# Layer 1: turning the softmax probabilities on VectorE and spreading them on ScalarE, in place of spread, TensorE turn and copy

## The reference, cut to what matters

```
x + _L1_attn_ref(_layernorm(x), w_qkv, b_qkv, w_o, b_o):
    q, k, v = split(x @ w_qkv.T + b_qkv)                # 8 heads, width 32
    scores = einsum('bhfc,bhtc->bhft', k, q)            # the key's rows f against the query's rows t
    scores = where(causal, scores, -10000)
    attn = softmax(scores, axis=-2)                     # over f
    vals = einsum('bhft,bhfc->bhtc', attn, v)
    out = vals @ w_o.T + b_o
```

## Time and profile before

| what | us |
|---|---|
| median of 3 runs | 2140.99 (2138.29 to 2141.76) |
| the profiled execution, its own time | 2136.47 |
| its span, first to last instruction | 2134.4 |
| PE busy | 2059.4 (96%) |
| DVE busy | 1308.7 (61%) |
| ACT busy | 683.7 (32%) |
| POOL busy | 248.3 (12%) |

### The profile page before, as it was taken

How to read it: one execution, slowest core, us unless ns; L and a number is a source line. 1 busy time by engine, 2 the same in 40 slices (tenths; PEclk the granted TensorE clock), 3 DMA queues, 4 the chain that set the end, 5 groups by cost and what they waited for, 6 DMA issues and landing times. The chain is left out here.

```text
span 2134.4 us, 33623 instructions
## 1 busy us (share of the span) xinstructions
PE 2059.4 (96%) x10660; PEld 1480.4 (69%) x10660; DVE 1308.7 (61%) x4451; ACT 683.7 (32%) x1861; POOL 248.3 (12%) x360
## 2 busy tenths in 40 slices
PE   7999999999999999999999999999899999779998
PEld 5778677777767778677777867777566666466665
DVE  3736547484654747456483755747577777677885
ACT  2333333333332433333242433333223223122222
POOL 0000000000000000000000000000233333133332
PEclk9999999999999999999999999999999999889999
DMA  7101000010000101001010000120100000000000
GB/s 289 31 15 31 23 24 30 24 30 24 24 20 24 30 24 30 24 24 30 14 37 16 30 23 24 30 86 1 45 1 1 1 0 29 0 1 21 21 15 25
DMA packets 51991, 62.14 MB, mean 29 GB/s; under 512 B 14193, under 2 KB 47665, under 8 KB 51042
## 3 DMA queue, kind: packets, MB, share of 16 engines
q1 hardware_dynamic: 51938, 61.46, 9.1%
HBM read 54.00 MB, written 4.29 MB: 27 GB/s over the span
## 5 line engine op out<-in xcount | busy, mean ns | idle before, releaser
L345 PE MATMUL psLane<-hid,WkT 128*128 128x289 f32 x1536 | 404.0, 408 | 0.0
L352 PE MATMUL psLane<-WvT,hid 128*128 128x384 f32 x1024 | 348.7, 486 | 0.0
L345 PEld LDWEIGHTS psLane<-hid,WkT 128*128 128x128 f32 x1536 | 284.1, 190 | 72.7
L352 PEld LDWEIGHTS psLane<-WvT,hid 128*128 128x128 f32 x1024 | 189.8, 190 | 109.7
L537 ACT ACTIVATE probs<-psLane,nmax 128x289 f32<-128x289 f32 x256 | 126.2, 498 | 423.6 <-DVE nmax L640 423.6
L505 ACT ACTIVATE KT<-psLane 96x289 f32<-96x289 f32 (+2 forms) x384 | 155.8, 406 | 153.3 <-PE psLane L345 151.0
L298 POOL TENSOR_TENSOR tails<-probs,unit 128x66 f32<-128x66 f32 x128 | 38.1, 297 | 1387.3 <-ACT probs L537 1387.3
L678 DVE MAX8 top<-work 128x8 f32<-128x257 f32 x512 | 180.3, 414 | 2.7
L335 PE MATMUL psLane<-xnT,WqT 128*128 128x128 f32 x1536 | 176.6, 275 | 0.0
L335 PEld LDWEIGHTS psLane<-xnT,WqT 128*128 128x128 f32 x1536 | 174.8, 192 | 0.3
L663 DVE TENSOR_TENSOR X<-X,psLane 128x512 f32 (+1 forms) x16 | 11.0, 689 | 261.6 <-PE psLane L417 261.6
(11 more groups left out here) (190 smaller groups left out, 3138.2 us busy)
## 6 DMA issues: line engine op xcount, KB each, us to landing
hid<-in_ctxT SPq DMA_DIRECT2D x64, 514.0 KB, 3.8
y<-X SPq DMA_DIRECT2D x16, 256.0 KB, 2.0
X<-in_x SPq DMA_DIRECT2D x1, 3840.0 KB, 14.9
WqT<-in_WqT SPq DMA_DIRECT2D x4, 768.0 KB, 11.4
WoT<-in_WoT SPq DMA_DIRECT2D x1, 3072.0 KB, 21.7
Vtail<-Vlat SPq DMA_DIRECT2D x128, 24.0 KB
w_qkv<-in_w_qkv SPq DMA_DIRECT2D x2, 1536.0 KB, 6.5
w_ffn<-in_w_ffn SPq DMA_DIRECT2D x2, 1024.0 KB, 8.0
```

The lines of the kernel that those rows point to most:

```text
L345: mm = pe.matmul(out[:, 0:S], WkT[:, c, P * k:P * k + P], hid[:, j, c, :], start=(c == 0), stop=(c == DC - 1))
L352: mm = pe.matmul(out[:, 0:KW], hid[:, j, c, P * s:P * s + P], WvT[:, c, :], start=(c == 0), stop=(c == DC - 1))
```

## The change: what it does

`turn_probs` is now DVE's last step: after the scaling it turns `p` (128x256) into the new buffer `turned` by DVE's transpose, which turns each 32x32 block by itself. As every batch and head is such a block, this is the turn that is needed. `spread_p` is now ACT's: four ACTIVATEs with function Copy and a scale of one number for each partition (a column of `jmask`) write `turned` to the block diagonal of `pT`. The eight turns of L1434 on PE, the four multiplies of L1562 on DVE and the copy of L1485 on ACT are gone. `values` takes over the wait for `v_ready`; `gate` waits for `s_filled` (the scores have read lane buffer 0) in place of `pt_filled`; DVE's `turn_probs` waits for `pt_ready` of the tile four earlier, which has read `turned`. In `SLOTS1`, `turn_probs` has DVE's old place 2.461, `spread_p` has 2.571, `values` has 2.769 in place of 2.919, and `evac_pt` is gone.

```diff
--- before.py
+++ after.py
@@ -850,7 +850,7 @@
     "gate": 0.000, "add_rest": 0.027, "mix": 0.173, "turn_mix": 0.485, "add_mix": 0.614, "stats1": 0.707,
     "rstd1": 0.773, "rows1": 0.929, "bias": 2.451, "turn1": 0.989, "xnT1": 1.045, "qkv": 1.310,
     "evac_qk": 1.590, "evac_v": 1.762, "spread_k": 1.808, "scores": 2.006, "mask": 2.056, "shift": 2.136,
-    "exps": 2.342, "spread_p": 2.461, "turn_probs": 2.571, "evac_pt": 2.710, "values": 2.919, "evac_ot": 2.919,
+    "exps": 2.342, "turn_probs": 2.461, "spread_p": 2.571, "values": 2.769, "evac_ot": 2.919,
     "project": 3.015, "add_proj": 3.074, "stats2": 3.162, "rstd2": 3.245, "rows2": 3.395, "turn2": 3.500,
     "xnT2": 3.539, "ffn": 3.877, "add_ffn": 3.989, "store": 3.989,}
 
@@ -1342,19 +1342,19 @@
         QK = sb("lane_QK", [P, LANES, 4, P])
         V = sb("lane_V", [P, LANES, EW])
         p = sb("lane_p", [P, LANES, EW])
+        turned = sb("lane_turned", [P, LANES, EW])
         gate = sb("gate1", [P, 1])
 
         n4, n5 = norm_sems(sem, "n4"), norm_sems(sem, "n5")
         names = ("gated", "gate_added", "mixed", "mix_turned", "mix_added", "bias_added", "qkv_filled", "v_ready",
                  "qk_ready", "kd_ready", "s_filled", "s_kept", "s_masked", "max_done", "s_shifted", "p_ready",
-                 "sum_done", "rinv_ready", "pd_ready", "pt_filled", "pt_ready", "av_filled", "p_scaled",
+                 "sum_done", "rinv_ready", "p_turned", "pt_ready", "av_filled", "p_scaled",
                  "ot_ready", "proj_filled", "proj_added", "ffn_filled", "ffn_added")
         s = {k: sem(f"l1_{k}") for k in names}
         out_done = sem("out_done")
 
         mixed = lambda u: lanes[:, u, 0, 0:D]
         Kd = lambda u: lanes[:, u, 0].rearrange("p (a j h k) -> p a j h k", a=2, j=TB, h=4)
-        Pd = lambda u: lanes[:, u, 0].rearrange("p (h j k) -> p h j k", h=EH, j=TB)
         pT = lambda u: lanes[:, u, 1]
         OT = lambda u: xnT[:, u, 0:EW // P]
         low = lambda u: ps[:, u, 0:512]
@@ -1427,15 +1427,9 @@
                                        Kd(u)[:, half, j], start=True, stop=True, tile_position=(0, L * j))
                 mm.then_inc(s["s_filled"], 1)
 
-            def turn_probs(t, u):
-                pe.wait_ge(s["pd_ready"], t + 1)
-                pe.wait_ge(s["v_ready"], t + 1)
-                for h in range(EH):
-                    mm = pe.transpose(ps[:, u, P * h:P * h + P], Pd(u)[:, h].rearrange("p j k -> p (j k)"), ident[:])
-                mm.then_inc(s["pt_filled"], 1)
-
             def values(t, u):
                 pe.wait_ge(s["pt_ready"], t + 1)
+                pe.wait_ge(s["v_ready"], t + 1)
                 for h in range(EH):
                     n, at = h // 4, L * (h % 4)
                     mm = pe.matmul(high(u)[at:at + L, P * n:P * n + P], V[:, u, L * h:L * h + L],
@@ -1456,7 +1450,7 @@
 
             over_lanes(pe, SLOTS1, STARTS1, {
                 "turn_mix": turn_mix, "turn1": lambda t, u: norm_turn(pe, n4, t, u, xn, high(u), ident), "qkv": qkv,
-                "scores": scores, "turn_probs": turn_probs, "values": values, "project": project,
+                "scores": scores, "values": values, "project": project,
                 "turn2": lambda t, u: norm_turn(pe, n5, t, u, xn, high(u), ident), "ffn": ffn})
 
         @block.scalar
@@ -1479,22 +1473,27 @@
                 act.wait_ge(s["s_shifted"], t + 1)
                 act.activation(p[:, u], p[:, u], ACT.Exp).then_inc(s["p_ready"], 1)
 
-            def evac_pt(t, u):
-                act.wait_ge(s["pt_filled"], t + 1)
+            def spread_p(t, u):
+
+                act.wait_ge(s["p_turned"], t + 1)
                 wait(act, s["av_filled"], t - LANES + 1)
-                act.activation(pT(u), ps[:, u, :], ACT.Copy).then_inc(s["pt_ready"], 1)
+                v = turned[:, u].rearrange("p (h q) -> p h q", h=EH)
+                for j in range(TB):
+                    ins = act.activation(pT(u).rearrange("p (h j q) -> p h j q", h=EH, j=TB)[:, :, j], v, ACT.Copy,
+                                         scale=jmask[:, j:j + 1])
+                ins.then_inc(s["pt_ready"], 1)
 
             def evac_ot(t, u):
                 act.wait_ge(s["av_filled"], t + 1)
                 act.activation(OT(u).rearrange("p n q -> p (n q)"), high(u)[:, 0:EW], ACT.Copy).then_inc(s["ot_ready"], 1)
 
-            over_lanes(act, SLOTS1, STARTS1, {"xnT1": evac_xnT(n4), "evac_qk": evac_qk, "exps": exps, "evac_pt": evac_pt,
+            over_lanes(act, SLOTS1, STARTS1, {"xnT1": evac_xnT(n4), "evac_qk": evac_qk, "exps": exps, "spread_p": spread_p,
                                      "evac_ot": evac_ot, "xnT2": evac_xnT(n5)})
 
         @block.vector
         def _(dve):
             def gate_crucial(t, u):
-                wait(dve, s["pt_filled"], t - LANES + 1)
+                wait(dve, s["s_filled"], t - LANES + 1)
                 v = mixed(u).rearrange("p (c j n) -> p c j n", c=DC, j=TB)
                 m = mask[:, :, bass.ts(t, P)].rearrange("p c (j n) -> p c j n", j=TB)
                 dve.tensor_tensor(v, m, blend[:, :, 1, bass.ts(t, TB)].unsqueeze(3).to_broadcast([P, DC, TB, L]),
@@ -1547,7 +1546,7 @@
                 dve.wait_ge(s["s_masked"], t + 1)
                 dve.tensor_reduce(small["rmax"][:, u, 0:EH], v, AX.X, ALU.max).then_inc(s["max_done"], 1)
 
-            def spread_p(t, u):
+            def turn_probs(t, u):
 
                 dve.wait_ge(s["p_ready"], t + 1)
                 v = p[:, u].rearrange("p (h k) -> p h k", h=EH)
@@ -1558,9 +1557,8 @@
                 dve.tensor_tensor(v, v, small["rinv"][:, u, 0:EH].unsqueeze(2).to_broadcast([P, EH, L]), ALU.mult)\
                     .then_inc(s["p_scaled"], 1)
                 dve.wait_ge(s["p_scaled"], t + 1)
-                for j in range(TB):
-                    ins = dve.tensor_scalar(Pd(u)[:, :, j], v, jmask[:, j:j + 1], None, ALU.mult)
-                ins.then_inc(s["pd_ready"], 1)
+                wait(dve, s["pt_ready"], t - LANES + 1)
+                dve.transpose(turned[:, u], p[:, u]).then_inc(s["p_turned"], 1)
 
             def add_projected(t, u):
                 dve.wait_ge(s["proj_filled"], t + 1)
@@ -1573,7 +1571,7 @@
 
             over_lanes(dve, SLOTS1, STARTS1, {
                 "gate": gate_crucial, "add_rest": add_rest, "mix": mix, "add_mix": add_mix, "stats1": stats(n4, before4), "rows1": rows(n4),
-                "evac_v": evac_v, "mask": mask_scores, "spread_p": spread_p,
+                "evac_v": evac_v, "mask": mask_scores, "turn_probs": turn_probs,
                 "add_proj": add_projected, "stats2": stats(n5, before5), "rows2": rows(n5), "add_ffn": add_ffn})
```

## The result

The changed kernel takes 2153.13 us (median of 5, 2152.06 to 2153.74) against 2138.29 us for the kernel before (5 runs, 2133.64 to 2141.76). The ratio is 1.0074, with a 95% interval from 1.0055 to 1.0092: slower by 15 us, where the forecast was +2.2 us and 2143.2, with a range up to 2151. The profiled execution took 2152.17 us with a span of 2150.4, 16.0 us above that of before.

A forecast was written before the change was run, and what follows sets the result against it. PE's own work, 14.35 us, plus one 0.63 us wait bounds a loop tile. Loop +5.4, opening -3.7, closing -2.3, clock +2.8 give +2.2 us on the profiled 2136.5, or 2143.2 as median; range 2136 to 2151.

The forecast's parts named there:

- What bounds the kernel, and the order: Layer 1 loop: PE's work plus one wait make the tile; `values` directly behind `turn2` waits for ACT; period 15.66 us.
- The prices: Loop tile: ACT's spread 1.66 us, DVE's transpose 0.42, PE's wait 2.24; +0.68 us per tile, +5.4 over eight.
- the sum: The prediction's added-up durations and waits: loop +5.4, opening -3.7, closing -2.3, together -0.6 us without a change of clock.
- Opening and closing: Layer 1 around the loop: opening -3.7 us from dropped turns and waits against new waits; closing -2.3 us.
- the old fall: Closing of the kernel before: one drop to the 1.2 GHz clock after 2110.0 to 2112.5 us, priced at 1.4 us.
- The clock: Loop: up to eight drops to the 1.2 GHz level at 1.4 us each; two were taken, +2.8 us.
- the two nearest stretches: Kernel before, PE little busy: 2110.0 to 2112.5 us, clock fell; 1917.5 to 1920.0, it did not.
- Rival 1: Loop: the clock falls in most tiles, six to eight falls, 2149 to 2152 us; chance 0.25.
- the whole thin stretch: Closing of the kernel before, 2110.0 to 2112.5 us: PE busy 1.09 of 2.5 us, all turns; the new wait was 2.24.

## Why the prediction was wrong

**What bounds the kernel, and the order.** Right. PE's own work and one wait make the loop tile, `values` lands directly behind `turn2`, and ACT's order (`xnT2`, spread, `evac_qk`) stands.

**The prices.** Right. Spread 1.69 us (forecast 1.66), DVE's turn 0.45 (0.42), wait 2.27 (2.24), tile without falls 15.65 to 15.67 (15.66). In the loop the queue behind ACT had its slack, and `scores` never waited. DVE's turn came 0.27 us later against `turn2` than the sum had it. `xnT2` covers that; where nothing does, it shows: with the multiplies left on DVE the wait was 1.35 us, not the 1.05 of the prediction.

**Opening and closing.** The opening was put 1.6 us too low: -2.1 without its fall. Its three largest new waits came out as forecast (0.78, 1.76 and 2.43 us for 0.8, 1.8 and 2.4). The smaller ones were too small: 0.90 us in front of the norm's turns at 1933.03 and 0.96 in front of `project` of tile 4, each put at 0.6, and 0.53 in front of `qkv` of tile 3 and 0.3 to 0.4 in front of a `turn_mix`, put at nothing. The closing was about right: 39.1 us in the run with one product, 3.6 below before. Of that 1.4 is the price of the old fall, which is gone there too, so 2.2 remains, and the forecast was 2.3. In the changed kernel the closing is 3.4 us longer than that. It begins with an `ffn` that has a fall, and later four waits of 1.1 to 1.4 us follow each other (L1435 is `values` of 14 and of 15, L1442 `project`, L834 `turn2` of 14):

```profile
2107.86 5.40 PE L1448 MATMUL psLane<-w_ffn,lane_xnT 128*128 128x512 f32 x8
...
2127.94 0.65 PE L1435 MATMUL psLane<-lanes,lane_V 128*32 128x128 f32 x16 [1.10 <-ACT lanes L1482]
2129.71 1.98 PE L1442 MATMUL psLane<-w_o,lane_xnT 128*128 128x512 f32 x4 [1.13 <-ACT lane_xnT L1488]
2132.81 0.64 PE L1435 MATMUL psLane<-lanes,lane_V 128*32 128x128 f32 x16 [1.11 <-ACT lanes L1482]
2134.83 0.66 PE L834 MATMUL psLane<-ident,lane_xn 128*128 128x128 f32 x4 [1.38 <-DVE lane_xn L818]
2135.32 3.54 PE L1442 MATMUL psLane<-w_o,lane_xnT 128*128 128x512 f32 x4
```

Two falls are the whole of the 3.4 us: `ffn` takes 5.40 us in place of 3.70, and the `project` at 2135.32 3.54 in place of 1.88. The clock was 0.53 and 0.52 over the 3.5 us from the start of each.

**The clock.** This is the step that failed: "I take two, since of the two nearest stretches one fell". One fall was put at 1.4 us and cost 1.6. The number was the miss: seven of eight in the loop, two in the closing, and one in the opening that was worth 2.6 us. So the term of the clock, put at +2.8 us, measured 17.4, or 16.0 net of the fall that the kernel before had in its closing. With the measured terms layer 1 adds up: waits in the loop +5.7, clock in the loop +11.4, opening -2.1 + 2.6, closing -3.6 + 3.4, together +17.4, where the traces show +17.5. (The part up to layer 1 was 1.5 us shorter in this execution, with nothing changed in it.) The mistake was to treat a stretch that recurs in each tile as so many separate draws, with the odds of two stretches that were seen once each. The tile is the same each time, and the wait stands at the same place in it. Rival 1 had the mechanism and 2149 to 2152 us, at a chance of 0.25. "The new wait is shorter by itself than the whole thin stretch" was no reason either: the turns in front of it belong to the thin stretch in both.

What decides between a fall in nearly every tile (2.27 and 1.91 us) and in none (1.57 us and below) can't be told from these runs. It isn't the length of the wait alone. The one tile that missed its fall in the changed kernel had the same wait of 2.27 us as its neighbours. Up to it the fall had come earlier against `values` from tile to tile: `values` took 0.65, 0.64, 0.71, 0.93, 1.08, 1.08 us and `ffn` 5.40, 5.40, 5.28, 5.06, 4.87, 4.74, then 0.64 and 3.70 in the tile without a fall, and 0.64 and 5.40 in the next. The kernel filled at tile 2 shows the same drift and one missed tile, at a wait of 2.37 us. With the spread ahead of `xnT2` `ffn` took 5.40 us in every tile and none was missed. And the four waits of the closing are the same there to 0.02 us as in the changed kernel, but its `project` took 1.88 us, at full clock. So the same waits brought a fall at one time and none at another; what settles which was not tried.

Of the two parts of the change, the new path (DVE's turn, ACT's spread) is a gain of 9 us if its reader stands behind `ffn`, and of 12 us with `turn2` moved as well. The place of `values` cost 25 to 26 us. In the traces of layer 1 it is 26.6, and over half of it is the clock: the changed kernel's falls come to 17.4 us, the two that are left with `values` behind `ffn` to about 3.

## What to carry to other kernels

When a step leaves the busiest engine, look at what it and its neighbours had been covering: here `ffn` had covered ACT's part for `values`, and the turn on TensorE had covered `xnT2` for `ffn`. In these runs a new wait on TensorE in the loop body had no fall of the clock in its steady tiles, or one in at least seven of eight. So price such a wait at both ends and don't take a number in between. If the wait can't be removed, a useless product in it can pay: 0.86 us of it per tile gave back 16 to 17 us of 2153.

## What the runs showed of the hardware

A DVE transpose of 128x256 fp32 in 32x32 blocks is one instruction of 446 ns, 35 ns above a reduction of the same tile (411 ns). An ACTIVATE of 128x256 with Copy and a per-partition scale takes 499 ns, and four in a row 1.69 us. In this loop the clock fell with PE waits of 1.91 and 2.27 us per tile and held with 0.69 and 1.35 us, each behind eight turns, and with 0.56 and 1.41 us that were left of the 2.27 behind products. Outside the loop a fall also came behind shorter waits that follow each other closely, of 0.95 and 1.11 us. Sixteen turns filled the gap as well as two products did (2139.8 and 2139.4 us). A fall on an `ffn` of eight records made it 5.40 us in place of 3.70.
